# A decoder layer's last feed-forward half product in two passes over the rows, with four raw weight slots

## The reference, cut to what matters

```python
logits = einsum(x, gate_w); routing_weights, _ = top_k(logits, 2)
h = relu(x @ up_w) ** 2                                  # 2048 wide
shared_out = h @ down_w
moe_out = (x @ fc1_w @ expert_w) * sum(routing_weights)  # 512 wide
routed_out = moe_out @ fc2_w
x = layernorm(x + layernorm(shared_out + routed_out, gamma, beta))
```

## Time and profile before

| | us |
|---|---|
| median of 3 runs | 730.73 (729.09 to 734.7) |
| the profiled execution's own time | 730.47 |
| its span | 728.7 |
| mean granted TensorE clock | 0.961 of full speed |
| PE busy | 647.7 (89%) |
| DVE busy | 409.5 (56%) |
| ACT busy | 282.0 (39%) |
| POOL busy | 156.5 (21%) |

### The profile page before, as it was taken

How to read it: one execution, slowest core, us unless ns; L and a number is a source line. 1 busy time by engine, 2 the same in 40 slices (tenths; PEclk the granted TensorE clock), 3 DMA queues, 4 the chain that set the end, 5 groups by cost and what they waited for, 6 DMA issues and landing times.

```text
span 728.7 us, 8538 instructions
## 1 busy us (share of the span) xinstructions
PE 647.7 (89%) x3080; PEld 523.5 (72%) x3080; DVE 409.5 (56%) x553; ACT 282.0 (39%) x386; POOL 156.5 (21%) x193
## 2 busy tenths in 40 slices
PE   4697798896679899999999999999999699999982
PEld 3586577673556578888888888878888488888861
DVE  6847789897795634544532233417777643223365
ACT  4545466554354424334322222423443222223222
POOL 3332466565512200000000000150223200000023
PEclk9899999999689999999999999999999899999997
DMA  9664425443733453333233344633555223233312
GB/s 345 205 202 119 131 73 170 142 140 95 235 118 94 173 147 111 89 89 113 73 102 102 98 145 132 185 120 87 159 183 174 61 74 109 93 101 101 112 48 87
DMA packets 95618, 93.56 MB, mean 128 GB/s; under 512 B 23776, under 2 KB 75232, under 8 KB 95584
## 3 DMA queue, kind: packets, MB, share of 16 engines
q1 hardware_dynamic: 91552, 78.44, 35.2%
q10 hardware_dynamic: 2304, 8.39, 3.5%
q0 software_dynamic: 1728, 6.29, 2.6%
HBM read 78.42 MB, written 10.49 MB: 122 GB/s over the span
## 4 chain that ended last, share of the span: by engine, by line
PE 57%; DVE 4%; DMA 2%; POOL 2%; ACT 1%; issue 0%; DVEq 0%; ACTq 0%; POOLq 0%
PE u_ps L1064 29%; PE acc L1076 26%; DVE act_sb L1229 1%; DMA d_raw<-in_L_ffn_down_w_dram 1%; DMA d_raw<-w_scratch 1%; DVE stat_f L1285 1%; DVE ffn L1278 1%; POOL rstd_f L1367 1%; POOL nbias L1371 1%; PE t_ps L1039 1%; PE t_ps L1040 1%; PE t_ps L1031 0%; POOL veps_f L1365 0%; DVE d_lo L1128 0%; ACT d_hi L1125 0%
## 5 line engine op out<-in xcount | busy, mean ns | idle before, releaser
L1064 PE MATMUL u_ps<-x2T_hi,u_hi 128*128 128x512 f32 x320 | 125.8, 393 | 7.2 <-DVE u_lo L1225 7.2
L1064 PE MATMUL u_ps<-x2T_lo,u_hi 128*128 128x512 f32 x320 | 125.2, 391 | 0.0
L1064 PE MATMUL u_ps<-x2T_hi,u_lo 128*128 128x512 f32 x320 | 125.2, 391 | 0.0
L1128 DVE TENSOR_TENSOR d_lo<-d_raw,d_hi 128x512 fp32r<-128x512 f32 x76 | 52.2, 691 | 124.6 <-ACT d_hi L1125 124.5
L1076 PE MATMUL acc<-d_hi,h_hi 128*128 128x512 f32 x304 | 119.4, 393 | 2.3 <-DVE d_lo L1128 2.2
L1076 PE MATMUL acc<-d_hi,h_lo 128*128 128x512 f32 x304 | 118.4, 390 | 0.0
L1076 PE MATMUL acc<-d_lo,h_hi 128*128 128x512 f32 x304 | 118.3, 389 | 0.0
L1125 ACT ACTIVATE d_hi<-d_raw 128x512 fp32r<-128x512 f32 x76 | 47.5, 630 | 124.6 <-PE acc L1076 87.5
L1064 PEld LDWEIGHTS u_ps<-x2T_hi,u_hi 128*128 128x128 f32 x320 | 60.6, 189 | 20.3 <-DVE u_lo L1225 7.6
L1064 PEld LDWEIGHTS u_ps<-x2T_hi,u_lo 128*128 128x128 f32 x320 | 60.5, 189 | 12.7
L1064 PEld LDWEIGHTS u_ps<-x2T_lo,u_hi 128*128 128x128 f32 x320 | 60.5, 189 | 12.5
(11 more groups left out here) (165 smaller groups left out, 1025.6 us busy)
## 6 DMA issues: line engine op xcount, KB each, us to landing
u_raw<-in_L_ffn_up_w_dram SPq DMA_DIRECT2D x32, 512.0 KB, 4.0
d_raw<-in_L_ffn_down_w_dram SPq DMA_DIRECT2D x64, 256.0 KB, 2.8
c_sb<-in_ctx_dram ACTq DMA_DIRECT2D x16, 512.0 KB, 4.7
x_sb<-in_x_dram SPq DMA_DIRECT2D x8, 512.0 KB, 5.0
res<-in_x_dram SPq DMA_DIRECT2D x8, 512.0 KB, 3.3
x_scratch<-res SPq DMA_DIRECT2D x8, 512.0 KB, 3.3
u_raw<-in_L_ffn_fc_w_dram SPq DMA_DIRECT2D x8, 512.0 KB, 3.7
d_raw<-w_scratch SPq DMA_DIRECT2D x16, 256.0 KB, 2.7
```

Source lines behind the costliest of these rows:

```text
L1064: mm = pe.matmul(u_ps[:, slot], s, v, start=(k == 0 and j == 0), stop=(k == KT - 1 and j == 2))
L1128: eng.tensor_tensor(d_slot(1, i), d_raw[:, i % 2], d_slot(0, i).bitcast(F32), ALU.subtract).then_inc(S["d_lo_done"], 1)
```

## The change

The last half product (batch 1, n = 1) is cut into two passes over the 20 items: first row tiles 0 and 1 (pass A), then 2 and 3 (pass B). Each pass loads and splits the whole weight half, so 20 more items are loaded and split; the number of matmuls stays the same. An item now has 6 matmuls instead of 12. Pass A does its last two items row by row, pass B its last eight. From pass A on there are four raw slots, the two of before and two in `act_sb`, which the first product no longer needs; a load there waits for the low part of the item four before. The layer norms of row tiles 0 and 1 move into pass B: on DVE behind items 5 and 7 (row tile 0) and 9 and 11 (row tile 1), on ACT behind items 9 and 13. Row tiles 2 and 3 come at the end as before. Two semaphores of the routing step are dropped or merged.

```diff
-        tail = lambda b, n: 2 * DH if (b, n) == (BATCH - 1, NH - 1) else DH // 2
+        passes = [(b, n, tuple(range(BT))) for b in range(BATCH) for n in range(NH)][:-1] + [(BATCH - 1, NH - 1, (0, 1)), (BATCH - 1, NH - 1, (2, 3))]
+        tail = lambda j: 2 * DH if j == len(passes) - 1 else DH // 2
...
-        TD = BATCH * NH * KD - 2 * DH
+        WIDE = (len(passes) - 2) * KD
+        d_in_slot = lambda i: i % 2 if i < WIDE else (i - WIDE) % 4
+        raw_slot = lambda i: d_raw[:, i % 2] if d_in_slot(i) < 2 else act_sb[:, i % 2]
+        TD = len(passes) * KD - 2 * DH
...
-            def load_d(b, n, k):
-                i = b * NB + n * KD + k
-                if i >= 2:
-                    sp.wait_ge(S["d_lo_done"], i - 1)
+            def load_d(j, k):
+                i, n = j * KD + k, passes[j][1]
+                if WIDE + 2 <= i < WIDE + 4:
+                    sp.wait_ge(S["h_lo_done"], BATCH * KD)
+                elif i >= 2:
+                    sp.wait_ge(S["d_lo_done"], i - (3 if i >= WIDE + 4 else 1))
...
@@ tensor
-                pe.wait_ge(S["ones_done"], 1)
...
-                for n in range(NH):
-                    for k in range(KD - tail(b, n)):
-                        for t in range(BT):
-                            second_product(b, n, k, t)
+                for j in [j for j, x in enumerate(passes) if x[0] == b]:
+                    n, rows = passes[j][1:]
+                    for k in range(KD - tail(j)):
+                        for t in rows:
+                            second_product(j, k, t)
...
-                    for t in range(BT):
-                        for k in range(KD - tail(b, n), KD):
-                            second_product(b, n, k, t)
+                    for t in rows:
+                        for k in range(KD - tail(j), KD):
+                            second_product(j, k, t)
@@ scalar
                     for k in range(2, KD):
-                        d_step(act, b, n, k, "hi")
+                        d_step(act, j, k, "hi")
...
+                        if j == len(passes) - 1 and k in (9, 13):
+                            final_norm(b * BT + (k - 9) // 4)
...
-                        if b == BATCH - 1 and n == NH - 1 and t:
+                        if j == len(passes) - 1 and t == BT - 1:
                             final_norm(b * BT + t - 1)
@@ vector
-                dve.tensor_copy(lg[:], both[:, :, 1]).then_inc(S["lgc_done"], 1)
-                dve.wait_ge(S["lgc_done"], b + 1)
+                dve.tensor_copy(lg[:], both[:, :, 1]).then_inc(S["lg_done"], 1)
+                dve.wait_ge(S["lg_done"], 2 * b + 1)
...
                     for k in range(2, KD):
-                        d_step(dve, b, n, k, "lo")
+                        d_step(dve, j, k, "lo")
...
-                        if n == NH - 1 and 6 <= k < 6 + BT:
+                        if j in (NH - 1, len(passes) - 2) and 6 <= k < 6 + BT:
                             half_stats(b * BT + k - 6, 0)
+                        if j == len(passes) - 1 and k in (5, 9):
+                            i = b * BT + (k - 5) // 4
+                            half_stats(i, 1)
+                            row_stats(i)
+                            scale_and_add(i)
+                        if j == len(passes) - 1 and k in (7, 11):
+                            last_stats(b * BT + (k - 7) // 4)
...
-            for t in range(BT):
+            for t in passes[-1][2]:
                 i = (BATCH - 1) * BT + t
                 half_stats(i, 1)
```

More of the change, by code:

```diff
@@ L914, in feed_forward @@
         DH = 4
-        tail = lambda b, n: 2 * DH if (b, n) == (BATCH - 1, NH - 1) else DH // 2
-        used_before = lambda j: sum(KD - tail(i // NH, i % NH) for i in range(j))
+        passes = [(b, n, tuple(range(BT))) for b in range(BATCH) for n in range(NH)][:-1] + [(BATCH - 1, NH - 1, (0, 1)), (BATCH - 1, NH - 1, (2, 3))]
+        tail = lambda j: 2 * DH if j == len(passes) - 1 else DH // 2
+        used_before = lambda j: sum(KD - tail(i) for i in range(j))
+        finished = lambda j, t: (passes[j][0] * NH + passes[j][1]) * BT + t + 1
         XO = KD - DH - KT
@@ L1065, in first_product, with second_product @@
                 mm.then_inc(S["u_ready"], 1)
-            def second_product(b, n, k, t):
-                i = b * NB + n * KD + k
+            def second_product(j, k, t):
+                i, (b, n, rows) = j * KD + k, passes[j]
                 pe.wait_ge(S["d_lo_done"], i + 1)
@@ L1074, in second_product @@
                 st = [h[:, k, t * P:(t + 1) * P] for h in (h_hi, h_lo)]
-                for j, (s, v) in enumerate(split_products(st, [d_slot(which, i) for which in range(2)])):
-                    mm = pe.matmul(acc[:, t], s, v, start=(k == 0 and j == 0), stop=(k == KD - 1 and j == 2))
+                for x, (s, v) in enumerate(split_products(st, [d_slot(which, i) for which in range(2)])):
+                    mm = pe.matmul(acc[:, t], s, v, start=(k == 0 and x == 0), stop=(k == KD - 1 and x == 2))
                 if k == KD - 1:
                     mm.then_inc(S["acc_ready"], 1)
-                elif t == BT - 1 and k < KD - tail(b, n):
+                elif t == rows[-1] and k < KD - tail(j):
                     mm.then_inc(S["d_used"], 1)
@@ L1119, in d_step @@
                     last = i - DH if i < TD else i - 2 * DH
-                    j, kj = last // KD, last % KD
-                    if kj >= KD - tail(j // NH, j % NH):
-                        eng.wait_ge(S["acc_ready"], (j + 1) * BT)
-                    else:
-                        eng.wait_ge(S["d_used"], used_before(j) + kj + 1)
-                eng.activation(d_slot(0, i), d_raw[:, i % 2], ACT.Copy).then_inc(S["d_hi_done"], 1)
+                    was, kw = last // KD, last % KD
+                    if kw >= KD - tail(was):
+                        eng.wait_ge(S["acc_ready"], finished(was, passes[was][2][-1]))
+                    else:
+                        eng.wait_ge(S["d_used"], used_before(was) + kw + 1)
+                eng.activation(d_slot(0, i), raw_slot(i), ACT.Copy).then_inc(S["d_hi_done"], 1)
             else:
                 eng.wait_ge(S["d_hi_done"], i + 1)
-                eng.tensor_tensor(d_slot(1, i), d_raw[:, i % 2], d_slot(0, i).bitcast(F32), ALU.subtract).then_inc(S["d_lo_done"], 1)
+                eng.tensor_tensor(d_slot(1, i), raw_slot(i), d_slot(0, i).bitcast(F32), ALU.subtract).then_inc(S["d_lo_done"], 1)
         @block.scalar
@@ L1193, in _ @@
                     else:
-                        d_step(act, b, 0, m - 2, "hi")
+                        d_step(act, b * NH, m - 2, "hi")
                         latent_hi(b, m)
-                for n in range(NH):
+                for j in [j for j, x in enumerate(passes) if x[0] == b]:
+                    n, rows = passes[j][1:]
                     last = b + 1 < BATCH and n == NH - 1
                     for k in range(2, KD):
-                        d_step(act, b, n, k, "hi")
+                        d_step(act, j, k, "hi")
                         if last and k >= XO + DH:
@@ L1203, in _ @@
                             split_u(w0 + WT + k - (KD - 2), k - (KD - 2), 16 * ((w0 + WT) // 2 + 1))
-                    if n + 1 < NH:
+                        if j == len(passes) - 1 and k in (9, 13):
+                            final_norm(b * BT + (k - 9) // 4)
+                    if j + 1 < len(passes) and passes[j + 1][0] == b:
                         for k in range(2):
-                            d_step(act, b, n + 1, k, "hi")
-                    for t in range(BT):
+                            d_step(act, j + 1, k, "hi")
+                    for t in rows:
                         act.wait_ge(S["acc_ready"], (b * NH + n) * BT + t + 1)
```

33 lines of the change are left out of this document (17 added, 16 removed).

## The result

The changed kernel takes 734.97 us (median of 20 runs, 732.01 to 739.85); the kernel before, run beside it, 731.4 (726.99 to 734.7). The medians lie 3.6 us apart. The estimated ratio is 1.0057, 95% interval 1.004 to 1.0073, which makes 4.2 us. So the change is slower by some 0.6%: the interval leaves 1 out, and it lies inside the 1% that the prediction took for no change. Forecast were 735.2 and 4.5 us.

A forecast was written before the change was run, and what follows sets the result against it. DVE's row of four norms was taken to set the end, hung on row tile 0's completion. With the change, 706.0 + 9.0 of waits and restarts + 18.2 gave 733.2, as a median 735.2 us; range 730 to 739.

The forecast's parts named there:

- The frame: End of the span as a sum: row tile completion, 6.55 us to its second statistics, 6.09 per further row tile, 5.6.
- norm turns: DVE and POOL's work per further row tile at the end, 6.09 us each; two gone save 12.2 us.
- X: Time at which row tile 2 is complete in the last half product: forecast 715.0, or 706.0 if PE never waits.
- The ceiling: Most the change could gain: with PE never waiting, the span would end at 724.2, 4.4 us sooner.
- Pass A costs nothing: First pass of the last half product: four slots give an item every 1.08 us, PE needs 1.36, so no waits.
- rival 3: Four loads in flight land late; from a landing of 4.0 us the loop decides: 738 to 744, chance 0.1.
- The term of DVE's split: DVE's low part of an item, taken at 0.70 us for each split in pass B.
- Item 14: Pass B: high part behind ACT's final norm of row tile 1, ready at 708.35; PE waits 2.4 us.
- Rival 2: PE's full clock is lost after a long wait, before the last row tile: 737 to 738.6 if unhidden, chance 0.12.
- POOL's part: POOL's instructions before ACT's final norm of row tile 1: 1.3 us undisturbed, plus 0.7 beside two DVE splits.
- Item 18: Pass B: its load waited for item 14's rest, then 2.9 us landing and splitting; PE waits 1.4 us.
- six restarts: PE resuming after each wait in pass B, 0.12 us each; they bring 8.3 us of waits to 9.0.

The follow-up runs named there:

- the short norms: The changed kernel with the norms of row tiles 0 and 1 computed on 16 of their 1024 columns only; ratio 0.9973 to the kernel before.

## Why the prediction was right

**The frame.** Two norm turns leave the end, and the end is X + 18.2: measured 75.52 - 57.58 = 17.94. The ceiling (X 49.1 with no wait) was reached to 0.3 us in the kernel without norms in pass B.

**Pass A costs nothing:** so it was. Landings did get longer, as the loads of `d_raw` show beside the earlier trace rows:

```profile
DMA to landing us min/median/max: 2.5/3.1/4.8
```

One load took 4.8 us, as rival 3 has it, but the median of 3.1 stayed below that rival's point of 4.0. The late one was item 4's of pass B. PE never waited for it, and the block behind item 5 began no more than 0.2 us later for it: item 5's high part could not have been made before PE was through with item 1, at 684.7, and was begun at 684.9. The windows of pass A and of the stretch from item 10 to 13 (columns as in the earlier trace rows; DMA share 0.62 in the first):

```profile
656.00:684.00 28.00, 28.00 (x125) 23.20 (x124) 16.66 (x26) 14.00 (x23) 0.00 (x0) 1.00 0.62 188
700.00:705.00 5.00, 5.00 (x16) 3.75 (x14) 2.36 (x6) 1.88 (x3) 1.65 (x3) 0.66 0.61 209
```

**The waits,** item by item. Mine were counted from the last matmul's turn of 0.23, the profile's begin 0.16 later, where it is modelled to end:

| before item | 6 | 8 | 10 | 12 | 14 | 18 |
|---|---|---|---|---|---|---|
| forecast | 1.2 | 0.2 | 2.9 | 0.2 | 2.4 | 1.4 |
| measured (profile's + 0.16) | 1.13 | 0 | 2.45 | 0 | 0.63 | 2.09 |

These are 6.3 us; with four restarts of 0.12, 6.8. X was 57.58 - 49.13 = 8.45 late, where I had 9.0. The missing 1.65 is the slow stretch, told under item 14.

- *Items 8, 10, 12.* The term of DVE's split was mis-sized at 0.70, its own length; two in a row take 1.20 (the chain has `d_lo` x2 at 1.20), 0.60 each. With the shorter last statistics (1.43, not 1.56) item 10 was ready 44.45 after the start, not 45.3.
- *Item 14.* Rival 2's event took place. After the gap of 2.29 us PE ran some five matmuls at the full clock, then those from 700.32 to 703.30 came at 0.43 us; the second window was granted 0.66, the lower of the two levels, 1.2 and not 2.4 GHz, for part of it. The 12 matmuls of items 10 and 11 took 4.46 us where 2.83 was their price at the full clock. That 1.6 us was taken out of item 14's wait, as the prediction had it ("the coming waits hide it"): in the change with six slots the clock stayed and that wait is 2.12. Item 14's readiness itself hung on ACT and POOL, at 50.9 where I had 52.2. Had row tile 3 been hit instead, it would have been seen in the end.
- *POOL's part.* From the last statistics' end at 701.16 to the final norm at 703.12 are 1.96 us; I had 1.3 + 0.7. Its timeline, beside the earlier trace rows:

```profile
701.24 0.52 POOL L1384 TENSOR_SCALAR veps_f<-mv_f 128x1 f32<-128x1 f32 x1 [4.11 <-DVE mv_f L1299]
701.84 0.87 POOL L1386 TENSOR_TENSOR rstd_f<-veps_f,neg_half 128x1 f32<-128x1 f32 x1
702.82 0.26 POOL L1390 TENSOR_SCALAR nbias<-mv_f,rstd_f 128x1 f32<-128x1 f32 x1
```

  The first two are 0.3 longer each than undisturbed, 0.52 for 0.19 and 0.87 for 0.55. DVE's two splits beside them:

```profile
701.07 1.24 DVE L1136 TENSOR_TENSOR u_lo<-d_raw,u_hi 128x512 fp32r<-128x512 f32 x2
```

  At 0.60 a split the first is over by about 701.7, and POOL's first instruction ends at 701.76; the second is over at 702.31, and POOL's second ends at 702.71. The Trainium skill (SBUF — State Buffer, Who interferes with whom) has a VectorE instruction with two SBUF inputs contend with a GpSimd instruction that reads SBUF, over ports that one of them locks for itself. I had made of it that POOL stands behind both splits at once, 0.7 more than I took. The trace fits one split of waiting for each of two POOL instructions, and not that reading.
- *Item 18.* The step was right (a late item 14 makes item 18 late), but its load took 3.53 us and not the 2.9 of the median. A thing that I had not looked at runs beside it: the stores of row tiles 0 and 1, 512 KB each, which SP issues from 706.60 on, right behind the loads of items 18 and 19. Without norms in pass B there is no store there, and the last two loads took 2.9 and 3.0 us. With a store about 1 us behind item 18's load it took 4.4 (one norm, ACT's behind item 13) and 4.1 (the change with six slots), but 2.8 with the short norms, where a store went out as close. So the stores are a candidate for the longer loads and no more; what lengthened this one stays open.

**How much of the closeness is luck.** Two things met in X. Item 14 was ready 1.3 us sooner than forecast (50.9 for 52.2), and item 18 followed it after 4.9 us instead of 4.2; the two errors of X's last chain nearly cancel (57.6 for 58.1). The sum has two slips of the same kind. Redone from its own times of readiness, its waits are 1.2, 0.3, 3.1, 0.3, 2.5 and 1.5, 8.9 us in all and not 8.3 (at item 10 the 0.16 of a matmul's tail had been counted to PE). And the six restarts do not add to them, because each wait ends at a time that PE doesn't set; only the last restart stays. Read straight from item 18, 713.3 + 1.36 + 0.16 + 0.12 = 714.9, the forecast's X is what it was. Last, the stage came out 3.7 us longer than before (75.5 against 71.8) where 4.6 was forecast; the median hit 735.2 to 0.2 us because the kernel before stands at 731.4 beside it and not at the 730.7 of three runs. What was right is the mechanism and its size within 1 us, not the last digit. Of the signs named, the waits before items 6, 10, 14 and 18, the longest at 10, ACT's norm ahead of 14, row tile 3 5.4 us behind row tile 2 and the last second statistics 6.09 us apart (718.33 and 724.42) all came; a spacing of 0.43 us came too, rival 2's sign, but not near the end.

**What I did not see** is how general the step from item 14 to item 18 is. I followed the held raw slot once, from 14 to 18, and took the other waits for the queue's alone. It did no harm here, because in the change the second block and ACT's norm are longer delays that swallow the ones from 6 to 10 and 14. Where one block is taken out it comes to light, and there my expectations failed twice by 3 us, the second time with ACT's moved norm as a part of it.

**What is not shown:** why the clock fell after 2.29 us and not after the 2.04 and 2.12 of the six-slot kernel. It fell after 1.87 us in the earlier trace rows as well, and in the two-slot kernel it stayed at 1.00 behind 3.18 and 2.97, so a gap's length alone doesn't order them.

## What to carry to other kernels

Work taken off the end and put into an in-order queue among short periodic steps costs what it overruns the consumer's lead by. Here blocks of 4.3 us made PE wait 1.0 and 2.3 us, and the same instructions in pieces of up to 2.2 us, with enough slots, 0.5 in all. So cut it by the lead, not by where its inputs are ready. A step that is late holds its input buffer too: count for each buffer which later load waits for it, all the way down the ring, and add slots before moving work about. And try the cheap half of a change by itself: four slots in one pass gave 0.3%, and 0.6% with the next row's work put into POOL's wait, where the two passes as built lost 0.6%.

## What the runs showed of the hardware

- Behind a gap of 2.29 us in PE's matmuls the full clock was lost once, for some 8 matmuls 0.43 us apart instead of 0.23. Behind single gaps of 1.93, 2.00, 2.04 and 2.12 us in the same stage of this and other kernels, and behind 3.18 and 2.97 us in the two-slot kernel, it stayed; there it fell later, behind two shorter ones (0.95 and 2.12).
- POOL's one-element instructions beside two splits in a row (two inputs, 0.60 us each) took 0.52 and 0.87 us instead of 0.19 and 0.55; beside a 128x1024 SCALAR_TENSOR_TENSOR of 1.28 us one takes about as long as that, 1.29 in the chain of the change.
- Two 128x512 splits or statistics in a row on DVE take 1.20 and 1.21 us in the chain, 0.60 each, where one alone takes 0.70.
- Loads of 256 KB (128 x 512 float32) with four in flight at a DMA share of 0.6 landed in 3.1 us in the median instead of 2.9, at most in 4.8 instead of 3.8 (`d_raw`'s loads). At 188 GB/s in pass A PE never waited for one.
